# Splitting the query rotation step and moving the residual loads ahead of the first output-projection weights in an 8-core attention + LoRA-FFN kernel

## What is computed

```python
def _L0_attn_ref(x, wq, wk, wv, wo):
    q = (x @ wq).reshape(B, S, 32, 128)
    k = (x @ wk).reshape(B, S, 8, 128)
    v = (x @ wv).reshape(B, S, 8, 128)
    q, k = _rope(q, pos), _rope(k, pos)
    scores = einsum('bqhgd,bshd->bhgqs', q by group, k) * 128 ** -0.5
    allowed = (j <= i) & (j > i - 1024)
    attn = softmax(where(allowed, scores, min))
    return einsum('bhgqs,bshd->bqhgd', attn, v) @ wo

x = layernorm(x + attn(x))
x = layernorm(x + (x @ W.T + b + picked_rank(x @ A.T @ B.T)))
```

## Time and profile before

| | us |
|---|---|
| three timed runs | 3612.88, 3622.35, 3747.82 (median 3622.35) |
| the profiled execution, device time | 3589.59 |
| its span, slowest core (core 2) | 3588.0 |
| spans of the 8 cores | 3556.8 to 3588.0 |
| mean granted TensorE clock of core 2 | 0.889 of full speed |
| attention of pass 1, about | 640 to 1320 |
| Wo stage of pass 1, about | 1320 to 1660 |
| attention and Wo stage of pass 2, about | 1690 to 2370, 2370 to 2710 |
| gate and dense layer, about | 2750 to 3588 |

### The profile page before, as it was taken

One profiled execution on the slowest core, in us unless ns is written; L12 is line 12 of the kernel. 1 busy time (PEld: TensorE's weight loads), 2 busy tenths in 40 slices (PEclk: granted clock), 3 DMA queues, 4 the chain that ended last, 5 costly groups with the idle time before them and its releaser, 6 DMA issues.

```text
span 3588.0 us, 41314 instructions; the slowest of 8 cores (3556.8 to 3588.0 us)
## 1 busy us (share of the span) xinstructions
PE 2668.0 (74%) x15474; PEld 1336.0 (37%) x15474; DVE 881.7 (25%) x2124; ACT 502.4 (14%) x934; POOL 225.4 (6%) x295
## 2 busy tenths in 40 slices
PE   4888888777777777775777777777774777757774
PEld 2334343444444443322444444433332333323331
DVE  1111111244444421112344444321112111111111
ACT  0000000232323220001323232310002000010001
POOL 1000100000000000000000000000000000000000
PEclk8999999999999988887999999988886778878897
DMA  8778877432232266773322322367772366676665
GB/s 128 125 130 137 144 137 129 83 56 51 48 60 48 50 104 94 95 102 61 56 51 48 59 48 50 57 106 101 105 99 36 47 94 94 90 163 94 97 91 145
DMA packets 177545, 315.37 MB, mean 88 GB/s; under 512 B 5688, under 2 KB 136904, under 8 KB 176328
## 3 DMA queue, kind: packets, MB, share of 16 engines
q0 software_dynamic: 175824, 295.89, 53.3%
q1 hardware_dynamic: 1528, 16.85, 1.4%
HBM read 591.81 MB, written 16.78 MB: 170 GB/s over the span
## 4 chain that ended last, share of the span: by engine, by line
PE 56%; DMA 20%; DVE 15%; issue 6%; ACT 2%; DVEq 1%; POOL 0%; ACTq 0%; POOLq 0%; SPq 0%
PE PS L560 12%; PE PS L966 11%; PE PS L753 11%; PE PS L388 8%; DMA SCR<-W_r 5%; DVE SCR L664 5%; DMA SCR<-wo_r 5%; DMA SCR<-wk_l 5%; DMA SCR<-wv_l 4%; PE PS L682 4%; PE PS L653 3%; PE PS L619 3%; DVE SCR L669 1%; DVE B L761 1%; DVE SCR L581 1%
## 5 line engine op out<-in xcount | busy, mean ns | idle before, releaser
L753 PE MATMUL PS<-SCR,B 128*128 128x512 bf16 x2048 | 507.0, 414 | 159.4 <-DVE B L761 81.8
L966 PE MATMUL PS<-SCR,B 128*128 128x512 bf16 x2048 | 511.6, 416 | 144.3 <-DMA SCR<-W_r 89.6
L388 PE MATMUL PS<-B,SCR 128*128 128x512 bf16 x2048 | 473.0, 391 | 90.6 <-DMA SCR<-wk_l 49.4
L560 PE MATMUL PS<-B,SCR 128*128 128x512 bf16 x2048 | 513.6, 397 | 0.0
L619 PE MATMUL PS<-B,SCR 128*128 128x512 bf16 (+1 forms) x768 | 234.2, 357 | 284.5 <-DVE SCR L669 148.8
L634 ACT ACTIVATE SCR<-PS 128x1152 bf16<-128x1152 f32 x256 | 289.6, 1131 | 862.1 <-PE PS L628 834.6
L753 PEld LDWEIGHTS PS<-SCR,B 128*128 128x128 bf16 x2048 | 212.7, 105 | 453.3 <-issue 253.6
L966 PEld LDWEIGHTS PS<-SCR,B 128*128 128x128 bf16 x2048 | 212.7, 105 | 440.1 <-issue 243.7
L388 PEld LDWEIGHTS PS<-B,SCR 128*128 128x128 bf16 x2048 | 201.4, 100 | 350.6 <-issue 135.2
L560 PEld LDWEIGHTS PS<-B,SCR 128*128 128x128 bf16 x2048 | 201.0, 103 | 204.9 <-issue 39.7
L619 PEld LDWEIGHTS PS<-B,SCR 128*128 128x128 bf16 x768 | 76.4, 103 | 398.0 <-issue 372.6
(11 more groups left out here) (92 smaller groups left out, 1479.0 us busy)
## 6 DMA issues: line engine op xcount, KB each, us to landing
SCR<-wq_l POOLq DMA_DIRECT2D x64, 1024.0 KB, 8.4
SCR<-wo_r POOLq DMA_DIRECT2D x64, 1024.0 KB, 10.5
SCR<-W_r POOLq DMA_DIRECT2D x64, 1024.0 KB, 10.2
SCR<-wk_l POOLq DMA_DIRECT2D x32, 1024.0 KB, 10.2
SCR<-wv_l POOLq DMA_DIRECT2D x32, 1024.0 KB, 9.5
B<-xo POOLq DMA_DIRECT2D x16, 1024.0 KB, 16.6
y<-B SPq DMA_DIRECT2D x8, 2048.0 KB, 8.6
B<-xh POOLq DMA_DIRECT2D x8, 1024.0 KB, 16.8
```

Source lines behind the costliest of these rows:

```text
L388: fns.append(lambda e, kc=kc, wsl=wsl, pjb=pjb, g=g: e.matmul(PS[:, pjb * 512: pjb * 512 + GRP], wsl[:, kc * 128:(kc + 1) * 128], xg_ap(g, ...
L560: fns.append(lambda e, kc=kc, wsl=wsl, xfm_ap=xfm_ap: e.matmul(PS[:, 7 * 512: 7 * 512 + PT], wsl[:, kc * 128:(kc + 1) * 128], xfm_ap(kc), ...
L753: fns.append(lambda e, ts=ts, kc=kc, wch=wch, kcl=kcl, DBt=DBt: e.matmul(bank(ts), DBt[:, kc * PT + ts * 128: kc * PT + (ts + 1) * 128], w ...
L966: fns.append(lambda e, tj=tj, t8=t8, dc=dc, wch=wch, dcl=dcl: e.matmul(bank(tj), z1_ap(dc, t8 * 128, 128), wch[:, dcl * 512:(dcl + 1) * 51 ...
```

## The change

There are two edits.

First, `emit_B` is cut into `emit_B1` (the ScalarE copy) and `emit_B2` (the rest), and at the end of a head `emit_B1(h + 1)` is called after the last query projection piece and before `tailT`, `emit_B2(h + 1)` where `emit_B` stood.

Second, in the Wo stage the early calls for c0 and c1 are gone: the four residual loads are recorded first, and every chunk, c0 and c1 too, is loaded inside the loop right ahead of its matmuls.

```diff
-            def emit_B(h):
+            def emit_B1(h):
+                hp = h % 2
+                qraw = scr.bf(QR[hp], PT)
+                P.do("act", lambda e, qraw=qraw: e.activation(
+                    qraw, PS[:, 7 * 512: 7 * 512 + PT], AF.Copy, scale=float(sm)),
+                    reads=[r_bank[7]], writes=[r_qraw[hp]])
+
+            def emit_B2(h):
                 hp = h % 2
                 qraw = scr.bf(QR[hp], PT)
                 qrot = scr.bf(QT[hp], PT)
-                P.do("act", lambda e, qraw=qraw: e.activation(
-                    qraw, PS[:, 7 * 512: 7 * 512 + PT], AF.Copy, scale=float(sm)),
-                    reads=[r_bank[7]], writes=[r_qraw[hp]])
                 P.do("pe", lambda e, qraw=qraw: e.matmul(
...
                     if h + 1 < HQ:
                         emit_A_piece(h + 1, s4, QS)
+                    if s4 == QS - 1 and h + 1 < HQ:
+                        emit_B1(h + 1)
                     if tailsT:
                         tailsT.pop(0)()
                     tailsT.append(tT)
                     tailsA.append(tA)
                     if s4 == QS - 1 and h + 1 < HQ:
-                        emit_B(h + 1)
+                        emit_B2(h + 1)
...
             r_xres.take(rxfm_r)
-            ch_sz = max(1, min(8, HQ, SLC_N // 512))
-            n_ch = HQ // ch_sz
-
-            def wo_chunk_load(ob, ch):
-                wch = scr.bf(SLC[ch % 2], ch_sz * 512)
-                P.do("gdma", lambda e, wch=wch, ob=ob, ch=ch: e.dma_start(
-                    out=wch[:, :].rearrange("p (s m) -> p s m", m=512),
-                    in_=wo_r[ob, ch * ch_sz:(ch + 1) * ch_sz].rearrange("s p m -> p s m"),
-                    max_dma_last_dim=8192),
-                    writes=[r_slc[ch % 2]])
-            wo_chunk_load(0, 0)
-            if n_ch > 1:
-                wo_chunk_load(0, 1)
             for ts_ in range(QS):
                 P.do("gdma", ld_cast(XR.bf(ts_ * D, D),
                                      xo[tok0 + ts_ * 128: tok0 + (ts_ + 1) * 128, :]),
                      writes=[r_xres])
+            ch_sz = max(1, min(8, HQ, SLC_N // 512))
+            n_ch = HQ // ch_sz
             for ob in range(OB):
                 lastw = None
                 for ch in range(n_ch):
-                    if not (ob == 0 and ch < min(2, n_ch)):
-                        wo_chunk_load(ob, ch)
                     wch = scr.bf(SLC[ch % 2], ch_sz * 512)
+                    P.do("gdma", lambda e, wch=wch, ob=ob, ch=ch: e.dma_start(
+                        out=wch[:, :].rearrange("p (s m) -> p s m", m=512),
+                        in_=wo_r[ob, ch * ch_sz:(ch + 1) * ch_sz].rearrange("s p m -> p s m"),
+                        max_dma_last_dim=8192),
+                        writes=[r_slc[ch % 2]])
```

More of the change, by code:

```diff
@@ L696, in build_program @@
                 emit_A_piece(0, j, QS)
-            emit_B(0)
+            emit_B1(0)
+            emit_B2(0)
             for h in range(HQ):
```

## The result

In 34 runs each, taken in turns, the changed kernel has a median of 3617.69 us and the kernel before one of 3603.79, a difference of 13.9 us. In some runs the cores of one die are granted a lower clock and the time is some per cent longer, so every ratio in this document compares the runs without that. The ratio of the two kernels is 1.004, with a 95% interval from 1.0023 to 1.0058: slower by 14 us (8 to 21), which is clear of no change though far inside 2%. The profiled execution took 3596.94 us, and its slowest core is core 6.

The account below looks back on a forecast made before the run. PE with the loads feeding it bounds the Wo stage. Split 0, load order 6.3 + 7.1 = 13.4, taken as 13 us, on 3622.35 gave 3635 us (+0.36%); effect range 7 to 27 us, time range 3600 to 3662.

Parts of the forecast that it names:

- Which edit costs: Whole kernel: splitting emit_B is worth 0, both ends 0; the order of Wo loads carries the sum, 13 us.
- The landing of c0: Wo stage start: c0 lands when xo4 did; PE waits 6.3 us (pass 1), 7.1 us (pass 2), 13 forecast.
- the lower end: Both Wo stage starts: if the slowest core fared like core 7, 3.3 us a pass, 6.6 us in all.
- What is late next: Wo stage after c0: c1 ready with 1.5 us or more to spare; c2 takes its 10.59 us as before.
- Extra idle ahead of c0: PE clock at c0: 6 to 7 us more idle costed at 0, at most 0.3 us a pass either way.
- The base of the sum: Whole-kernel time: median of three timed runs, 3622.35 us, plus 13 gives 3635 us, or +0.36%.
- The signs that I had listed: POOL: four xo then two wo_r loads; PE: c0 waits 6 to 7 us, wo_r waits 18, about 90 us.
- A: Start of Wo stage: c0's load is hidden after all, +0 to +7 us, 3622 to 3629; chance 0.13.
- B: Opening burst of Wo loads: landings not in issue order, +27 us or somewhat more, 3649; chance 0.08.
- C: All 16 Wo blocks: each gets a second wait of 4.8 us, over 2% slower, about +89 us, 3711; chance 0.03.
- D: Whole kernel: faster by over 2%, the split worth more than its 29.7 us of waits; chance 0.02.

Follow-up runs that it names:

- split_only: The kernel before with only emit_B cut into emit_B1 and emit_B2, loads in the old order; ratio 1.0001 (0.9984 to 1.0019).
- order_only: The kernel before with only the residual loads first and c0 and c1 inside the loop, emit_B whole; ratio 1.0039 (1.0017 to 1.0061).
- x4_c1_c0: The kernel before with Wo loads ordered xo1 to xo4, c1, c0, so c0 is sixth and last; ratio 1.0058 (1.0029 to 1.0087).

## Why the prediction was right, and where it was not

**Which edit costs: right.** The two edits were read apart as one without an effect and one with all of it, and split_only and order_only show both, 1.0001 and 1.0039.

**The landing of c0: the mechanism right, the sum for both passes somewhat too large.** The step was that c0 lands when xo4 did, since four residual loads and one chunk have gone by either way. It landed 33.2 and 32.2 us after the burst began, where xo4 had taken 33.4 and 34.7. I forecast new idle of 6.3 and 7.1 us for the slowest core and 13 us in all. The slowest core shows waits of 6.28 and 7.10. That the digits agree is luck: these include 1.06 us of idle each that this core had before, so that 11.3 us are new, and the slowest core is now core 6, while my rows are from core 2, which shows 5.99 and 5.46. The mean core has 9.4 new, and core 3 only 2.7, below the 6.6 that I had from core 7 as the lower end. The time moved by 14 us (8 to 21), an interval that holds 9.4 as well as 13.

**What is late next: right.** c1 was no wait, in the changed kernel; the wait for c2 stayed, 3.42 and 6.36 us on core 6 where I had said 4 to 5; the stage's length stayed within what it varies by. Extra idle ahead of c0 cost little at the clock, 0.2 us in pass 1 and 0.6 in pass 2, where I had allowed 0.3 a pass: the clock stood at its lower level there in both kernels.

**The base of the sum: wrong.** The step that failed is "3622.35 + 13 = 3635". The shift held within its interval, what I added it to did not. The median of three runs, 3622.35, stood for the kernel before, and in 34 runs its median is 3603.79, 18.6 us lower. One of the three, 3747.82, lay far above the others, so that the median was the higher of the two that remained (3612.88 and 3622.35); three runs do not fix the base to better than the whole effect. Read as an absolute time, 3635 is 17 us too high and makes a rise of 31 us of one of 14; the same 13 us on 3603.79 would have given 3617, where 3617.69 was measured. The profiled execution of 3589.6, which I had before me, spoke for a lower base, and I named it without drawing on it.

**The signs that I had listed.** The four loads at the burst's start, two chunks behind, none under head 30, the copy's waits at 29.7 us: as foreseen. The count of waits for `wo_r` rose from 16 to 18 on cores 1 and 5 and from 19 to 21 on core 6, which had three more than core 2 already before; there c3, just late, has a wait of 0.17 us of its own. The total of 90 us that I gave holds for core 4 alone (89.6); the mean is 81.7.

**The rivals.** A (hidden) came true in part on cores 3 and 7, whose waits are 1.65 to 4.20 us. B (no order in landing) is refuted by the six places of c0, as far as loads of this size in one queue go. C (lateness in every block) did not occur in any order, even with c0 some 13 us late in each pass. D is refuted with split_only.

## What to carry to other kernels

When loads on one queue are reordered, list when each is wanted and what lands in front of it. In these runs a load was free until its place in the burst passed its deadline, and beyond that one more load ahead of it cost 7.4 us a pass, for it feeds the engine that sets the time. Here four residual tiles, wanted 29 us later, stood in front of weights that were wanted at once. And look at the waits that recur before the one that occurs once: one buffer more and banks in turn were worth 213 us where the order was worth 14.

## What the runs showed of the hardware that I had not expected

A wait of PE of 4 to 6 us costs more than its length. The 32 matmuls of a chunk took 7.07 us with PE kept busy, at a granted clock of 0.99 to 1.00, and mostly 8.4 to 8.9 us after such waits, when the clock had been granted at half for a part of them. Between 3 and 4 us it goes either way: 8.75 us after a wait of 3.42 (changed kernel, core 6), 7.07 after one of 3.79 (x4_c1_c0, core 1). So 71.8 us of waits gave back 97.6 us of stage, and some 150 us of them gave 204.

With a load always under way behind the one awaited, landing took little longer: `wo_r` landed in 10.5 us at the median with two buffers, 11.4 with three, and 11.7 to 13.1 in the four executions with three and alternate banks, at 143 GB/s moved instead of 99. The stage had looked bound by its loads; it was bound by when they were asked for.
